# Attention slots of a four-layer kernel: the norms turned one tap earlier, one rotation step on GpSimd, and GpSimd's order changed

## The chip, the cores and the metric

One core of a Trainium2 chip. The metric is the device time of one execution of the whole program, in microseconds; lower is better. The kernel before takes 2851.93 us (median of 3 runs, 2851.05 to 2853.13).

## What is computed

Four post-norm layers on x of shape (4, 512, 512) in float32: a pooled-attention layer, a dense gated FFN, a lagged attention with 16 heads of 128, and a mixture of 8 experts. The change lies in the third. Cut to what matters:

```python
q, k, v = silu(x @ Wq), silu(x @ Wk), silu(x @ Wv)      # z = x @ Wz, a = x @ Wa, b = x @ Wb
q, k, v = (causal_dwconv(u, w) for u, w in ...)          # 4 taps along the sequence
q = q * cos + rot_half(q) * sin                          # rot_half: (-second half, first half)
k = k * cos + rot_half(k) * sin
q = q / maximum(norm(q), 1e-12); k = k / maximum(norm(k), 1e-12)
for s in range(4):                                       # lags
    attn = einsum('bshd,bshd->bsh', q, lag(k, s)) * scale
    out = out + (attn * sigmoid(lag(a, s) * b))[..., None] * lag(v, s)
out = out * rsqrt(mean(out * out) + eps) * norm_w * silu(z)
x = layernorm(x + out @ Wout)
```

## The kernel before

**Slots.** The lagged attention runs as 64 slots, slot f.s = 4 * head + batch (`f.head`, `f.b`). A slot works on four steps at once: f projects and convolves its own step, l1 is the step one slot behind (squares, norms, scores), l2 two behind (mixture, gate, output projection), l3 three behind (its output is added to `x_tok`). Every engine has its own program, written out by hand in the order in which it runs; semaphores join them. Nothing reorders an instruction at run time.

**TensorE in a slot**, in order: 12 matmuls of 512 columns into bank A (first halves of q and k), 12 into B (second halves), the squares and values of l1 turned, `mix(l2)`, `score(l1)`, 12 into A (v), 12 into B (z of l1), 12 of the output projection. The v block waits for the three taps on c1 (`s_c1`), since A must be free, the z block for those on c2 (`s_c2`), and the next slot's first matmul for those on cv (`s_cv`).

**VectorE in a slot**: `accumulate(l3)` four times, `probabilities(l2)` (gate times query norms, out `lag_prob`), three taps on c1, the sums of squares (`norm_sums`, lines L3217 and L3220), the first tap on c2, `gated_output`, two taps on c2, `gains` (L3191), `turn_norms` (L3225), `y_low`, cross2 = c1 * sin (L3483), cross1 = c2 * sin (L3489), three taps on cv, and r1 = r1 - cross1 (L3500).

**GpSimd in a slot**: `band_of_query(l2)` (L2952, the query norms times a band mask, in place), the low parts of the next head's weights (`split_head`, L2941/L2944; two matrices where f.b is 1 or 2, one where it is 3, none where it is 0), the power -1/2 of the norms (L3082), r1 = c1 * cos (L3085), the issue of a DMA that adds l2's squares in DRAM (L2961), r2 = c2 * cos (L3090), r2 = r2 + cross2 (L3093), and the sum of both squares (L3095).

**The query norms travel.** The 1/norm of q is wanted along the other axis, in every partition. `turn_norms` writes it turned; SyncE stores it to DRAM with five small DMAs (`store_query`), waits for their landing, and loads it back broadcast to 128 partitions (`load_query`). Two lines say who waits for it:

```python
def band_of_query(st):
    pool.wait_ge(s_query, st.s * 96 + 96)
...
def probabilities(st):
    dve.wait_ge(s_band, st.s + 1 + (st.s > WHOLE))
```

SyncE's queue then moves r1 and r2 into `rot_q` and `rot_k` by four DMAs (partition halves are regrouped), for the score of the next slot.

Of the kernel before, what the change touches and what calls it, by code (L numbers as in the profile page):

```python
# [86 lines left out]
def until(eng, sem, value):  # L87

    if not isinstance(value, int) or value > 0:
        eng.wait_ge(sem, value)  # L90
# [1700 lines left out]
def layers(nc, mem, a, lag_b, saved, query_norm, square_sums, store):  # L1791
# [16 lines left out]
    with phase(nc) as ctx:  # L1808
# [200 lines left out]
        with nc.Block() as block:  # L2009
            @block.sync  # L2010
            def _(sp):
# [93 lines left out]
                for f, l1, l2, l3 in slots():  # L2105
# [26 lines left out]
                    if l1 and l1.s < BY_ROW:  # L2132
# [3 lines left out]
                        load_query(l1)  # L2136
                    sp.wait_ge(s_rotated, 3 * f.s + 3)
                    until(sp, s_s, f.s)
                    sp.dma_start(rot_q[0:64, 0:SEQ], r1[0:64, :]).then_inc(s_move1, 16)
                    sp.dma_start(rot_k[0:64, :], r1[64:128, :]).then_inc(s_move1, 16)  # L2140
                    sp.wait_ge(s_cos, f.s * 3 + 3)
                    sp.dma_start(rot_q[64:128, 0:SEQ], r2[0:64, :]).then_inc(s_move2, 16)
                    sp.dma_start(rot_k[64:128, :], r2[64:128, :]).then_inc(s_move2, 16)
                    if f.s == 0:
# [345 lines left out]
            def _(act):  # L2490
# [242 lines left out]
                for f, l1, l2, l3 in slots():  # L2733
# [14 lines left out]
                    act.activation(A, A, ACT.Silu).then_inc(s_silu, 1)  # L2748
                    until(act, s_cos, f.s * 3 - 2)
                    until(act, s_rotated, 3 * f.s - 2)  # L2750
                    act.wait_ge(s_silu, f.s * 3 + 1)
# [6 lines left out]
                    act.activation(B, B, ACT.Silu).then_inc(s_silu, 1)  # L2758
                    until(act, s_cos, f.s * 3 - 1)
                    until(act, s_rotated, 3 * f.s - 1)  # L2760
                    act.wait_ge(s_silu, f.s * 3 + 2)
# [172 lines left out]
            def _(pool):  # L2934
# [132 lines left out]
                pool.wait_ge(s_rotation, 32)  # L3067
                for f, l1, l2, l3 in slots():
                    if l2 and l2.s < BY_ROW:
                        band_of_query(l2)  # L3070
                    if f.b and f.head + 1 < HEADS:
                        split_head(f.head + 1, 1 - f.wbuf, SPLIT_AT[f.b])
                    elif f.b == 1:
                        experts.sums(pool, 0)
                        experts.split_lo(pool, 0, 0)
                    elif f.b == 2:
                        pool.wait_ge(s_op, f.head * BATCH * TPB)
                        experts.split_lo(pool, 0, 1)
                        experts.split_lo(pool, 0, 2)
                    if l1:  # L3080
                        pool.wait_ge(s_n2, 3 * l1.s + 2)
                        pool.tensor_tensor(norms[l1.rbuf][:, 0:2 * TPB], norm2, half[:, 0:2 * TPB], ALU.pow).then_inc(s_rn, 1)  # L3082
                    pool.wait_ge(s_c1, f.s * TAPS + TAPS)
                    until(pool, s_move1, f.s * 32)
                    pool.tensor_tensor(r1, c1, cos, ALU.mult).then_inc(s_cos, 1)  # L3085
                    if l2 and l2.s < BY_ROW:
                        add_squares(l2)
                    pool.wait_ge(s_c2, f.s * TAPS + TAPS)
                    until(pool, s_move2, f.s * 32)
                    pool.tensor_tensor(r2, c2, cos, ALU.mult).then_inc(s_cos, 1)  # L3090
                    pool.wait_ge(s_cos, f.s * 3 + 2)
                    pool.wait_ge(s_rotated, 3 * f.s + 1)
                    pool.tensor_tensor(r2, r2, cross2, ALU.add).then_inc(s_cos, 1)  # L3093
                    pool.wait_ge(s_sqr, f.s * 2 + 2)
                    pool.tensor_tensor(squares[0], squares[0], squares[1], ALU.add).then_inc(s_pair, 1)  # L3095
                    if f.s == END - 1:
                        mean_root(0)
                    elif f.s == END:
                        with_residual(0)
# [62 lines left out]
            def _(dve):  # L3162
# [279 lines left out]
                for f, l1, l2, l3 in slots():  # L3442
# [22 lines left out]
                    if l2:  # L3465
                        gated_output(l2)
                    tap(1, f, B, c2, 2, s_c2)
                    tap(1, f, B, c2, 3, s_c2)
                    if l1:
                        gains(l1)  # L3470
                        if f.s == END:
                            probabilities(l1)
                            sum_features(2, OP0)
                        turn_norms(l1)
                    if f.s == 1:
# [3 lines left out]
                    dve.wait_ge(s_c1, f.s * TAPS + TAPS)  # L3479
                    until(dve, s_cos, 3 * f.s)  # L3480
                    if f.s == 0:
# [5 lines left out]
                    dve.wait_ge(s_c2, f.s * TAPS + TAPS)  # L3487
                    until(dve, s_rotated, 3 * f.s)
                    dve.tensor_tensor(cross1, c2, sin, ALU.mult).then_inc(s_rotated, 1)  # L3489
# [6 lines left out]
                    if f.s >= END - 1:  # L3496
                        mean_squares(f.s - (END - 1))
                    dve.wait_ge(s_cos, f.s * 3 + 1)
                    dve.wait_ge(s_rotated, 3 * f.s + 2)
                    dve.tensor_tensor(r1, r1, cross1, ALU.subtract).then_inc(s_rotated, 1)  # L3500
                    if f.s == END:
# [249 lines left out]
```

## Time and profile before

| what | value |
|---|---|
| median of 3 runs | 2851.93 us (2851.05 to 2853.13) |
| the profiled execution's own time | 2859.97 us |
| its span | 2858.2 us |
| busy: PE, PEld, DVE, ACT, POOL | 2821.6, 2322.7, 2307.8, 1445.7, 1683.5 us |
| granted TensorE clock | 0.997 of full speed |
| attention slots | from about 747 to 1830 us |
| 823 to 1762 us: PE, DVE, ACT, POOL busy of 939 us | 933.2, 893.0, 525.4, 614.3 us |

PE busy is a union of overlapping matmuls: one is recorded as 0.39 us long and the next starts 0.227 us after it, so a short pause between two does not show in the busy share. The starts of matmuls tell more.

### The profile page before, as it was taken

To read this page: it belongs to the slowest core of one execution; us is meant where nothing else is said; L and a number is where in the kernel's file an instruction comes from. 1 tells how busy PE (TensorE), PEld (TensorE's weight loads), DVE (VectorE), ACT (ScalarE), POOL (GpSimd) and SP (SyncE) were. 2 spreads that over 40 slices of the span, in tenths; PEclk is the share of its full clock that TensorE was granted. 3 is DMA by queue.
4 is the path that set the end of the run, shared out by engine and by line. 5 is a ranking of instruction groups with operands and counts; after the bars stand their busy time and mean duration, and the time that the engine had idled before them with its cause. 6 is when DMAs were issued, how large, how long until landed. Compare 5 with 4: busy or idle time off the path is not lost.

```text
span 2858.2 us, 39883 instructions
## 1 busy us (share of the span) xinstructions
PE 2821.6 (99%) x13234; PEld 2322.7 (81%) x13234; DVE 2307.8 (81%) x3268; ACT 1445.7 (51%) x2653; POOL 1683.5 (59%) x1204
## 2 busy tenths in 40 slices
PE   9999999999999999999999999899999999999998
PEld 7888888888788888888888888777778887888886
DVE  7899587777899999999999999877667777666665
ACT  6656333333655555555555555564545445444443
POOL 7787233333466666666666666756545556556554
PEclk9999999999999999999999999999999999999999
DMA  3000000000334444444444443321111111211111
GB/s 138 1 23 25 12 19 27 30 27 26 121 98 101 97 97 97 101 97 97 99 99 106 106 104 86 108 74 52 52 45 52 60 45 58 83 45 60 52 52 45
DMA packets 99347, 193.98 MB, mean 68 GB/s; under 512 B 15688, under 2 KB 24264, under 8 KB 98120
## 3 DMA queue, kind: packets, MB, share of 16 engines
q1 hardware_dynamic: 90760, 175.70, 20.7%
q0 software_dynamic: 8384, 15.73, 4.2%
q8 instruction: 108, 1.77, 0.3%
q14 instruction: 95, 0.78, 0.1%
HBM read 133.32 MB, written 24.51 MB: 55 GB/s over the span
## 4 chain that ended last, share of the span: by engine, by line
PE 69%; DVE 13%; DMA 7%; issue 6%; POOL 2%; SPq 2%; ACT 1%; DVEq 0%; ACTq 0%; POOLq 0%
PE OP L45 7%; PE OP L47 7%; PE OP L46 7%; DVE lag_c L3170 4%; DMA lag_query<-query_norm_scratch 4%; DMA query_norm_scratch<-lag_turned 3%; PE S L1470 3%; PE S L1472 3%; PE S L1471 3%; PE A L45 2%; PE A L1470 2%; PE A L1471 2%; PE A L1472 2%; PE A L47 2%; PE A L46 2%
## 5 line engine op out<-in xcount | busy, mean ns | idle before, releaser
L1546 DVE SCALAR_TENSOR_TENSOR x_tok<-OP,expert_weight,x_tok 128x512 f32<-128x512 f32 x252 | 188.1, 748 | 137.4 <-PE OP L47 137.3
L1425 POOL TENSOR_TENSOR middle_w_lo<-second_raw,middle_w_hi 128x512 fp32r<-128x512 f32 (+1 forms) x96 | 143.9, 1500 | 210.2 <-ACT middle_w_hi L1420 210.2
L1518 POOL TENSOR_TENSOR middle_in_lo<-middle_slot,middle_in_hi 128x512 fp32r<-128x512 f32 x128 | 168.7, 1318 | 131.8 <-ACT middle_in_hi L1514 130.9
L3082 POOL TENSOR_TENSOR lag_norms<-lag_norm,minus_half 128x8 f32<-128x8 f32 x63 | 105.0, 1667 | 192.1 <-DVE lag_norm L3220 192.0
L45 PE MATMUL A<-xT_hi,lag_w_hi 128*128 128x512 f32 x512 | 209.9, 410 | 4.0 <-DVE lag_cv L3170 1.7
L45 PE MATMUL B<-xT_hi,lag_w_hi 128*128 128x512 f32 x516 | 204.6, 396 | 5.0 <-DVE lag_c L3170 2.9
L47 PE MATMUL B<-xT_hi,lag_w_lo 128*128 128x512 f32 x516 | 201.4, 390 | 0.0
L46 PE MATMUL B<-xT_lo,lag_w_hi 128*128 128x512 f32 x516 | 201.1, 390 | 0.0
L47 PE MATMUL A<-xT_hi,lag_w_lo 128*128 128x512 f32 x512 | 199.8, 390 | 0.0
L46 PE MATMUL A<-xT_lo,lag_w_hi 128*128 128x512 f32 x512 | 199.7, 390 | 0.0
L45 PE MATMUL OP<-middle_down_hi,middle_in_hi 128*128 128x512 f32 x496 | 193.6, 390 | 1.9 <-POOL middle_down_lo L1445 1.7
L47 PE MATMUL OP<-middle_down_hi,middle_in_lo 128*128 128x512 f32 x496 | 193.1, 389 | 0.0
L46 PE MATMUL OP<-middle_down_lo,middle_in_hi 128*128 128x512 f32 x496 | 193.0, 389 | 0.0
L1425 POOL TENSOR_TENSOR middle_w_lo<-middle_raw,middle_w_hi 128x512 fp32r<-128x512 f32 (+1 forms) x96 | 155.0, 1618 | 64.5 <-ACT middle_w_hi L1420 62.5
L2748 ACT ACTIVATE A<-A 128x512 f32<-128x512 f32 x64 | 37.2, 582 | 278.7 <-PE A L47 278.7
L1263 DVE TENSOR_TENSOR x_tok<-OP,x_tok 128x512 f32<-128x512 f32 x188 | 128.9, 689 | 54.7 <-PE OP L47 54.5
L3170 DVE SCALAR_TENSOR_TENSOR lag_c<-A,lag_conv,lag_c 128x511 f32<-128x511 f32 (+2 forms) x192 | 143.2, 746 | 18.0 <-ACT lag_c L2752 13.2
L1470 PE MATMUL S<-xT_hi,middle_w_hi 128*128 128x512 f32 x384 | 150.4, 392 | 1.5 <-ACT middle_slot L1503 0.8
L1508 ACT ACTIVATE middle_slot<-middle_slot 128x512 f32<-128x512 f32 x128 | 80.8, 632 | 138.9 <-DVE middle_slot L1527 138.8
L1472 PE MATMUL S<-xT_hi,middle_w_lo 128*128 128x512 f32 x384 | 149.5, 389 | 0.0
L2952 POOL TENSOR_TENSOR lag_query<-lag_query,lag_band 128x524 f32<-128x524 f32 x62 | 75.5, 1218 | 122.5 <-DMA lag_query<-query_norm_scratch 122.5
L3170 DVE SCALAR_TENSOR_TENSOR lag_cv<-A,lag_conv,lag_cv 128x511 f32<-128x511 f32 (+2 forms) x192 | 143.0, 745 | 4.6
(706 smaller groups left out, 9286.3 us busy)
## 6 DMA issues: line engine op xcount, KB each, us to landing
lag_raw<-in_head_weights SPq DMA_DIRECT2D x64, 256.0 KB, 4.3
lag_b_row<-lag_b_scratch SPq DMA_DIRECT2D x64, 256.0 KB, 3.3
lag_rot_q<-lag_r SPq DMA_DIRECT2D x128, 128.0 KB, 2.4
lag_rot_k<-lag_r SPq DMA_DIRECT2D x128, 128.0 KB, 2.4
middle_down_raw<-in_expert_down SPq DMA_DIRECT2D x32, 512.0 KB, 3.4
lag_query<-query_norm_scratch SPq DMA_DIRECT2D x62, 262.0 KB
square_sums_scratch<-head_squares POOLq DMA_DIRECT2D x60, 256.0 KB, 4.2
middle_raw<-in_expert_in SPq DMA_DIRECT2D x32, 384.0 KB, 3.0
```

The source lines that it names most:

```text
L45: pe.matmul(out, lh, rh, start=first and k == 0, stop=False)
L46: pe.matmul(out, lh, rl, start=False, stop=False)
L47: done = pe.matmul(out, ll, rh, start=False, stop=last and k == n - 1)
L1263: dve.tensor_tensor(row, self.down_bank(q, n), row, ALU.add).then_inc(self.s_acc, 1)
L1425: pool.tensor_tensor(self.w_lo[q % 2][:, out], self.raw[q % 2][:, of], f32(self.w_hi[q % 2][:, out]), ALU.subtract).then_inc(self.s_wlo, 1)
L1470: pe.matmul(out, w_hi, hi[:, k, :], start=first and k == 0, stop=False, skip_group_check=not first)
L1471: pe.matmul(out, w_hi, lo[:, k, :], start=False, stop=False, skip_group_check=not first)
L1472: done = pe.matmul(out, w_lo, hi[:, k, :], start=False, stop=k == 1, skip_group_check=not first)
L1518: pool.tensor_tensor(self.inner_lo[q % 3][t], self.slot((1, 3)[t], q), f32(self.inner_hi[q % 3][t]), ALU.subtract).then_inc(self.s_lo, 1)
L1546: dve.scalar_tensor_tensor(row, self.down_bank(v, n), self.expert_weight[:, e:e + 1], row, op0=ALU.mult, op1=ALU.add).then_inc(self.s_acc, 1)
L3082: pool.tensor_tensor(norms[l1.rbuf][:, 0:2 * TPB], norm2, half[:, 0:2 * TPB], ALU.pow).then_inc(s_rn, 1)
L3170: dve.scalar_tensor_tensor(out[:, shift:], src[:, 0:SEQ - shift], wj, out[:, shift:], op0=ALU.mult, op1=ALU.add).then_inc(done, 1)
```

## The change

Four things. (1) VectorE turns the norms of l1 between the second and the third tap on c2, where before it did so after the third tap and the gains. (2) r1 = r1 - cross1 moves from VectorE, behind the cv taps, to GpSimd, behind r2 = r2 + cross2; `s_cos` now counts four steps a slot and `s_rotated` two, and all waits follow. (3) GpSimd splits the next head's weights first and masks the query norms after, and issues the DMA of squares after r2 = c2 * cos instead of before it. (4) SyncE moves r2 first and r1 after.

```diff
@@ SyncE
-                    sp.wait_ge(s_rotated, 3 * f.s + 3)
+                    sp.wait_ge(s_cos, f.s * 4 + 3)
                     until(sp, s_s, f.s)
+                    sp.dma_start(rot_q[64:128, 0:SEQ], r2[0:64, :]).then_inc(s_move2, 16)
+                    sp.dma_start(rot_k[64:128, :], r2[64:128, :]).then_inc(s_move2, 16)
+                    sp.wait_ge(s_cos, f.s * 4 + 4)
                     sp.dma_start(rot_q[0:64, 0:SEQ], r1[0:64, :]).then_inc(s_move1, 16)
                     sp.dma_start(rot_k[0:64, :], r1[64:128, :]).then_inc(s_move1, 16)
-                    sp.wait_ge(s_cos, f.s * 3 + 3)
-                    sp.dma_start(rot_q[64:128, 0:SEQ], r2[0:64, :]).then_inc(s_move2, 16)
-                    sp.dma_start(rot_k[64:128, :], r2[64:128, :]).then_inc(s_move2, 16)
@@ GpSimd
+                    if f.b and f.head + 1 < HEADS:
+                        split_head(f.head + 1, 1 - f.wbuf, SPLIT_AT[f.b])
                     if l2 and l2.s < BY_ROW:
                         band_of_query(l2)
-                    if f.b and f.head + 1 < HEADS:
-                        split_head(f.head + 1, 1 - f.wbuf, SPLIT_AT[f.b])
...
                     pool.tensor_tensor(r1, c1, cos, ALU.mult).then_inc(s_cos, 1)
-                    if l2 and l2.s < BY_ROW:
-                        add_squares(l2)
                     pool.wait_ge(s_c2, f.s * TAPS + TAPS)
                     until(pool, s_move2, f.s * 32)
                     pool.tensor_tensor(r2, c2, cos, ALU.mult).then_inc(s_cos, 1)
-                    pool.wait_ge(s_cos, f.s * 3 + 2)
-                    pool.wait_ge(s_rotated, 3 * f.s + 1)
+                    if l2 and l2.s < BY_ROW:
+                        add_squares(l2)
+                    pool.wait_ge(s_cos, f.s * 4 + 2)
+                    pool.wait_ge(s_rotated, 2 * f.s + 1)
                     pool.tensor_tensor(r2, r2, cross2, ALU.add).then_inc(s_cos, 1)
+                    pool.wait_ge(s_rotated, 2 * f.s + 2)
+                    pool.tensor_tensor(r1, r1, cross1, ALU.subtract).then_inc(s_cos, 1)
@@ VectorE
                     tap(1, f, B, c2, 2, s_c2)
+                    if l1:
+                        turn_norms(l1)
                     tap(1, f, B, c2, 3, s_c2)
                     if l1:
                         gains(l1)
...
-                        turn_norms(l1)
...
-                    dve.wait_ge(s_cos, f.s * 3 + 1)
-                    dve.wait_ge(s_rotated, 3 * f.s + 2)
-                    dve.tensor_tensor(r1, r1, cross1, ALU.subtract).then_inc(s_rotated, 1)
```

GpSimd's order before, from the rotation of one slot to that of the next, where the next one splits two matrices (`lag_w_lo10` and `lag_w_lo11` are the low parts, `lag_query` the masked query norms, `lag_norms0` the power):

```order
L3085 TENSOR_TENSOR lag_r1<-lag_c1,lag_cos 128x512
L2961 DMA square_sums_scratch<-head_squares 128x512
L3090 TENSOR_TENSOR lag_r2<-lag_c2,lag_cos 128x512
L3093 TENSOR_TENSOR lag_r2<-lag_r2,lag_cross2 128x512
L3095 TENSOR_TENSOR lag_square0<-lag_square0,lag_square1 128x512
L2952 TENSOR_TENSOR lag_query<-lag_query,lag_band 128x524
L2941 TENSOR_TENSOR lag_w_lo10<-lag_raw0,lag_w_hi10 128x512
L2941 TENSOR_TENSOR lag_w_lo11<-lag_raw1,lag_w_hi11 128x512
L3082 TENSOR_TENSOR lag_norms0<-lag_norm2,minus_half 128x8
```

The same place in the changed kernel:

```order
L3085 TENSOR_TENSOR lag_r1<-lag_c1,lag_cos 128x512
L3088 TENSOR_TENSOR lag_r2<-lag_c2,lag_cos 128x512
L2961 DMA square_sums_scratch<-head_squares 128x512
L3093 TENSOR_TENSOR lag_r2<-lag_r2,lag_cross2 128x512
L3095 TENSOR_TENSOR lag_r1<-lag_r1,lag_cross1 128x512
L3097 TENSOR_TENSOR lag_square0<-lag_square0,lag_square1 128x512
L2941 TENSOR_TENSOR lag_w_lo10<-lag_raw0,lag_w_hi10 128x512
L2941 TENSOR_TENSOR lag_w_lo11<-lag_raw1,lag_w_hi11 128x512
L2952 TENSOR_TENSOR lag_query<-lag_query,lag_band 128x524
L3082 TENSOR_TENSOR lag_norms0<-lag_norm2,minus_half 128x8
```

One instruction more stands there (the new L3095), the two splits stand ahead of the mask instead of behind it, and the DMA's issue has changed places with r2 = c2 * cos.

VectorE's order before, from the c2 taps to the end of a slot:

```order
L3207 SCALAR_TENSOR_TENSOR O<-O,lag_norm,lag_zs 128x512
L3170 SCALAR_TENSOR_TENSOR lag_c<-B,lag_conv,lag_c 128x510
L3170 SCALAR_TENSOR_TENSOR lag_c<-B,lag_conv,lag_c 128x509
L3191 SCALAR_TENSOR_TENSOR lag_gate<-lag_gate,S 128x524
L3225 STREAM_TRANSPOSE lag_turned<-lag_norms 128x32
L3212 TENSOR_TENSOR lag_y_lo<-O,lag_y_hi 128x512
L3483 TENSOR_TENSOR lag_cross<-lag_c,lag_sin 128x512
L3489 TENSOR_TENSOR lag_cross<-lag_c,lag_sin 128x512
L3170 SCALAR_TENSOR_TENSOR lag_cv<-A,lag_conv,lag_cv 128x511
L3170 SCALAR_TENSOR_TENSOR lag_cv<-A,lag_conv,lag_cv 128x510
L3170 SCALAR_TENSOR_TENSOR lag_cv<-A,lag_conv,lag_cv 128x509
L3500 TENSOR_TENSOR lag_r<-lag_r,lag_cross 128x512
```

And in the changed kernel:

```order
L3209 SCALAR_TENSOR_TENSOR O<-O,lag_norm,lag_zs 128x512
L3172 SCALAR_TENSOR_TENSOR lag_c<-B,lag_conv,lag_c 128x510
L3227 STREAM_TRANSPOSE lag_turned<-lag_norms 128x32
L3172 SCALAR_TENSOR_TENSOR lag_c<-B,lag_conv,lag_c 128x509
L3193 SCALAR_TENSOR_TENSOR lag_gate<-lag_gate,S 128x524
L3214 TENSOR_TENSOR lag_y_lo<-O,lag_y_hi 128x512
L3486 TENSOR_TENSOR lag_cross<-lag_c,lag_sin 128x512
L3492 TENSOR_TENSOR lag_cross<-lag_c,lag_sin 128x512
L3172 SCALAR_TENSOR_TENSOR lag_cv<-A,lag_conv,lag_cv 128x511
L3172 SCALAR_TENSOR_TENSOR lag_cv<-A,lag_conv,lag_cv 128x510
L3172 SCALAR_TENSOR_TENSOR lag_cv<-A,lag_conv,lag_cv 128x509
```

The transpose stands one tap and the gains earlier, and the last row is gone.

## Rows read from the trace of the kernel before

**Rows 1.** The page, part 1: busy us, share of the span, instructions.
```profile
PE 2821.6 (99%) x13234; PEld 2322.7 (81%) x13234; DVE 2307.8 (81%) x3268; ACT 1445.7 (51%) x2653; POOL 1683.5 (59%) x1204
```

**Rows 2.** The waits of all engines: us in total, times, longest us.
```profile
PEld B L45 <- DVE lag_c L3170: 14.9, 32, 1.0
PEld A L45 <- DVE lag_cv L3170: 12.6, 29, 0.5
```

**Rows 3.** Timeline of PE: the first matmuls of slots 3, 4, 46, 60, 62.
```profile
806.58 0.39 PE L45 MATMUL A<-xT_hi,lag_w_hi 128*128 128x512 f32 x1
...
822.86 0.39 PE L45 MATMUL A<-xT_hi,lag_w_hi 128*128 128x512 f32 x1
...
1527.32 0.50 PE L45 MATMUL A<-xT_hi,lag_w_hi 128*128 128x512 f32 x1
...
1761.39 0.47 PE L45 MATMUL A<-xT_hi,lag_w_hi 128*128 128x512 f32 x1 [0.17 <-DVE lag_cv L3170]
...
1794.60 0.50 PE L45 MATMUL A<-xT_hi,lag_w_hi 128*128 128x512 f32 x1
```

**Rows 4.** Timeline of PE in slot 46: the last v matmul and the first of z.
```profile
1538.06 0.39 PE L47 MATMUL A<-xT_hi,lag_w_lo 128*128 128x512 f32 x1
1538.29 0.50 PE L45 MATMUL B<-xT_hi,lag_w_hi 128*128 128x512 f32 x1
```

**Rows 5.** Timeline of DVE in slot 46, and the c1 taps of slot 60.
```profile
1530.76 1.68 DVE L3199 TENSOR_TENSOR lag_prob<-lag_gate,lag_query 128x524 f32<-128x524 f32 x1 [0.38 <-POOL lag_query L2952]
1532.36 2.31 DVE L3170 SCALAR_TENSOR_TENSOR lag_c<-A,lag_conv,lag_c 128x511 f32<-128x511 f32 x3
1534.59 0.68 DVE L3217 TENSOR_REDUCE lag_norm<-OP 128x8 f32<-128x512 f32 x1
...
1535.38 0.75 DVE L3170 SCALAR_TENSOR_TENSOR lag_c<-B,lag_conv,lag_c 128x511 f32<-128x511 f32 x1
...
1536.71 1.52 DVE L3170 SCALAR_TENSOR_TENSOR lag_c<-B,lag_conv,lag_c 128x510 f32<-128x510 f32 x2
...
1538.76 0.21 DVE L3225 STREAM_TRANSPOSE lag_turned<-lag_norms 128x32 f32<-128x32 f32 x1
...
1539.45 1.78 DVE L3483 TENSOR_TENSOR lag_cross<-lag_c,lag_sin 128x512 f32<-128x512 f32 x1
1541.15 0.68 DVE L3489 TENSOR_TENSOR lag_cross<-lag_c,lag_sin 128x512 f32<-128x512 f32 x1
1541.75 2.31 DVE L3170 SCALAR_TENSOR_TENSOR lag_cv<-A,lag_conv,lag_cv 128x511 f32<-128x511 f32 x3
1543.98 0.82 DVE L3500 TENSOR_TENSOR lag_r<-lag_r,lag_cross 128x512 f32<-128x512 f32 x1
...
1765.85 2.32 DVE L3170 SCALAR_TENSOR_TENSOR lag_c<-A,lag_conv,lag_c 128x511 f32<-128x511 f32 x3 [0.59 <-ACT lag_c L2752]
```

**Rows 6.** Timeline of POOL in slot 46, to the mask of slot 47.
```profile
1529.42 1.21 POOL L2952 TENSOR_TENSOR lag_query<-lag_query,lag_band 128x524 f32<-128x524 f32 x1 [1.98 <-DMA lag_query<-query_norm_scratch]
1530.59 3.00 POOL L2941 TENSOR_TENSOR lag_w_lo<-lag_raw,lag_w_hi 128x512 fp32r<-128x512 f32 x2
1535.55 1.67 POOL L3082 TENSOR_TENSOR lag_norms<-lag_norm,minus_half 128x8 f32<-128x8 f32 x1 [1.96 <-DVE lag_norm L3220]
1537.21 1.29 POOL L3085 TENSOR_TENSOR lag_r<-lag_c,lag_cos 128x512 f32<-128x512 f32 x1
1538.45 0.89 POOL L2961 DMA_DIRECT2D square_sums_scratch<-head_squares  x1
1539.09 1.58 POOL L3090 TENSOR_TENSOR lag_r<-lag_c,lag_cos 128x512 f32<-128x512 f32 x1
1541.37 1.62 POOL L3093 TENSOR_TENSOR lag_r<-lag_r,lag_cross 128x512 f32<-128x512 f32 x1 [0.70 <-DVE lag_cross L3483]
...
1546.52 1.22 POOL L2952 TENSOR_TENSOR lag_query<-lag_query,lag_band 128x524 f32<-128x524 f32 x1 [2.28 <-DMA lag_query<-query_norm_scratch]
```

More of the change, by code:

```diff
@@ L2748, in _ @@
                     act.activation(A, A, ACT.Silu).then_inc(s_silu, 1)
-                    until(act, s_cos, f.s * 3 - 2)
-                    until(act, s_rotated, 3 * f.s - 2)
+                    until(act, s_cos, f.s * 4 - 3)
+                    until(act, s_rotated, 2 * f.s - 1)
                     act.wait_ge(s_silu, f.s * 3 + 1)
@@ L2758, in _ @@
                     act.activation(B, B, ACT.Silu).then_inc(s_silu, 1)
-                    until(act, s_cos, f.s * 3 - 1)
-                    until(act, s_rotated, 3 * f.s - 1)
+                    until(act, s_cos, f.s * 4 - 2)
+                    until(act, s_rotated, 2 * f.s)
                     act.wait_ge(s_silu, f.s * 3 + 2)
@@ L3068, in _ @@
                 for f, l1, l2, l3 in slots():
+                    if f.b and f.head + 1 < HEADS:
+                        split_head(f.head + 1, 1 - f.wbuf, SPLIT_AT[f.b])
                     if l2 and l2.s < BY_ROW:
                         band_of_query(l2)
-                    if f.b and f.head + 1 < HEADS:
-                        split_head(f.head + 1, 1 - f.wbuf, SPLIT_AT[f.b])
-                    elif f.b == 1:
+                    if f.head + 1 == HEADS and f.b == 1:
                         experts.sums(pool, 0)
                         experts.split_lo(pool, 0, 0)
-                    elif f.b == 2:
+                    elif f.head + 1 == HEADS and f.b == 2:
                         pool.wait_ge(s_op, f.head * BATCH * TPB)
@@ L3479, in _ @@
                     dve.wait_ge(s_c1, f.s * TAPS + TAPS)
-                    until(dve, s_cos, 3 * f.s)
+                    until(dve, s_cos, 4 * f.s - 1)
                     if f.s == 0:
@@ L3487, in _ @@
                     dve.wait_ge(s_c2, f.s * TAPS + TAPS)
-                    until(dve, s_rotated, 3 * f.s)
+                    until(dve, s_cos, 4 * f.s)
                     dve.tensor_tensor(cross1, c2, sin, ALU.mult).then_inc(s_rotated, 1)
```

## The prediction

> **What bounds the kernel now.** I read the page's busy shares first, then the waits, then the starts of matmuls, then the timelines of VectorE and GpSimd in one slot. TensorE is busy 99% of the span [rows 1], but matmuls overlap in the records, so that number hides short pauses; VectorE's 81% is an average over four layers. The waits name the pauses: before the z block TensorE waits for the c2 taps, and before a slot's first matmul for the cv taps, together 27.5 us, both VectorE's work [rows 2]. How much can be had is read from starts. The quiet slot 3 lasts 822.86 - 806.58 = 16.28 us; from slot 3 to slot 62 there are 59 slots in 1794.60 - 806.58 = 988.02 us, 16.75 us each [rows 3]. The same matmuls at the quiet slot's pace would take 59 * 16.28 = 960.5 us, so 27.5 us is what the slots lose. A late start also costs about 0.11 us beyond the wait: the first matmul after one is 0.50 us long where 0.39 is usual [rows 3, 4].
>
> Why VectorE is late shows in slot 46, which starts at 1527.32 and splits two matrices. Two things add up.
>
> First, a loop through DRAM. The mask of the query norms ends at 1529.42 + 1.21 = 1530.63 [rows 6]; VectorE multiplies with it, goes through the taps, and turns the next norms at 1538.76, 8.13 us later [rows 5]; from there to the next mask's start, through store and load, are 1546.52 - 1538.76 = 7.76 us, and GpSimd had been idle 2.28 us when the data came [rows 6]. With the mask's 1.22 us the loop takes 17.11 us against TensorE's 16.28.
>
> Second, blocking between VectorE and GpSimd. `lag_prob` takes 1.68 us while GpSimd splits weights [rows 5, 6]. cross2 takes 1.78 us where its twin cross1 takes 0.68: it ends at 1541.23, 0.56 us after GpSimd's r2 = c2 * cos, which ends at 1539.09 + 1.58 = 1540.67 [rows 5, 6]. And r2 = r2 + cross2 takes 1.62 instead of 1.29 us beside cross1. So where both inputs lie in SBUF, one engine waits until the other's instruction is over, while the taps, which read a bank, keep 0.75 us each. The Trainium skill says the same on its page "SBUF — State Buffer", section "Who interferes with whom": the port pair is an exclusive lock, taken by a VectorE instruction with two SBUF inputs against a GpSimd one that reads SBUF. It weighs against giving GpSimd yet another SBUF operation, but a page's rule has no duration here; the sum below takes the blocked times from the rows.
>
> **The change, costed.** Let E be the time from a slot's start to the end of its mask; slot 46 has E = 3.31. Everything after it follows from start-to-start distances in [rows 5, 6].
>
> VectorE from E: `lag_prob` starts 0.13 us later. In the new order GpSimd is idle then, since the splits are done, so it costs 0.62 to the next start instead of 1.60 (1532.36 - 1530.76): a full 1.0 us off the slots that split. The c1 taps start at E+0.75, the sums of squares at +2.23 = E+2.98, the first c2 tap at +0.79 = E+3.77, the second at +1.33 = E+5.10, the moved transpose at +0.67 = E+5.77, the third tap 0.13 later (its 0.21 us less the usual 0.08 of overlap) and over at E+6.65; z can start 0.06 after that, E+6.71. The transpose needs the power, which ends at E+3.94+1.67 = E+5.61, so it has 0.16 us to spare and waits for nothing.
>
> When z wants to start: 1538.06 + 0.23 - 1527.32 = 10.97 us into slot 46, less the 0.11 of restart in it: 10.86 [rows 3, 4]. So E up to 4.15 costs nothing. An early E gains nothing either, since ScalarE gives c1 only 1765.85 - 1761.39 = 4.46 us into a slot [rows 3, 5], as if E were 3.7.
>
> The loop through DRAM, new: 5.77 + 7.76 + 1.22 = 14.75 us, against 17.11. It no longer binds, with 1.5 us to spare.
>
> GpSimd's own loop, new. From E: the power at +3.94, r1 = c1 * cos at +5.60, r2 = c2 * cos at +6.84 (c2 is ready at 6.65), the DMA's issue at +8.09. That holds GpSimd 0.93 us (from 1538.45 to 1540.67 - 1.29), to +9.02. Meanwhile VectorE reaches cross2 at 6.65 + 1.10 = +7.75 (1539.45 - 1538.23 less the transpose's 0.12), is blocked to +8.13, and ends it at +8.69 and cross1 at +9.29. So r2 = r2 + cross2 works from about +9.2, not +9.02. Then one instruction each 1.25 us: the new r1 = r1 - cross1 at +10.45, squares +11.70, split +12.95, split +14.20, mask +15.45, over at +16.67. With one split the loop is 15.42 us, with none 14.17. The price of the new subtraction, 1.25, is taken from its neighbours' start distance (1.24 between the two instructions from 1537.21); if cross1 blocked it like the addition it would be 1.58.
>
> Chain the slots of a head, each starting P after the one before, and E' = E + loop - P. f.b = 0: E is 3.7 at its floor. f.b = 1: 3.7 + 16.67 - 16.28 = 4.09, z at 10.80, no loss. f.b = 2: 4.09 + 0.39 = 4.48, z at 11.19 instead of 10.86, loss 0.33 + 0.11 = 0.44, P = 16.72. f.b = 3, one split: 3.18, no loss. Back at f.b = 0 GpSimd would give 1.6 and DRAM 3.7 + 14.75 - 16.28 = 2.2, both under the floor. The cv taps end at E + 9.21 + 2.31 = 16.0 even for f.b = 2, before TensorE wants bank A at 16.7: that wait goes in all slots, since the subtraction of 0.82 us [rows 5] is off VectorE and cross2 is blocked for 0.4 instead of 1.1 us.
>
> Losses left: 14 heads * 0.44 = 6.2 us. Gain: 27.5 - 6.2 = 21.3 us; I take 1 us off for transfers that come unusually late, so 20.
>
> At nothing I cost three things. The moves of r1 and r2: r1 is done at E+11.74 = 16.2 even at f.b = 2, where it is 1543.98 + 0.82 - 1527.32 = 17.5 now, so the score is served earlier; without that, a late move would stall TensorE one for one. The sum of squares ends 0.5 us later (17.5) and is turned after 24 matmuls of the next slot, about 22. The slots beyond 62 and the tail: nothing, perhaps a gain of 1 us, as VectorE has one instruction less there.
>
> All of this is in the profiled execution, whose span is 2858.2 and own time 2859.97 us; the median shown is 8 us lower, and I apply the 20 us to the median: 2851.9 - 20 = 2832 us.
>
> **Rivals.** (a) TensorE reaches its pace in all slots: if GpSimd's loop is 0.2 us shorter per slot than I work out (for instance if the addition does not wait for cross1, 9.02 instead of 9.2), f.b = 2 loses little or nothing, gain 27 us, time 2825.
>
> (b) The loop is 0.3 us longer, the subtraction blocked to 1.58: f.b = 1 has E = 4.4 and loses 0.35, f.b = 2 has 4.7 and loses 0.69. 14 heads * 1.04 = 14.6 us lost, gain 13, time 2839.
>
> (c) Slower. The issue of the squares' DMA now falls on cross2 and cross1 (+8.09 to +9.29), where today it falls on taps and gains. No row shows an issue beside an instruction with two SBUF inputs. If those hold it up, it starts at +9.29, ends at +10.2 instead of 9.2, and the loop is 1.0 us longer: f.b = 1: E = 5.1, loss 1.05; f.b = 2: 5.4, loss 1.39; f.b = 3: 4.2, loss 0.14. 14 * 2.58 = 36 us, against 27.5 now: 9 us slower, 2861. It decides from about 0.7 us on. The bounds of the issue's price are 0.93 (free, as now) and 1.93; I take 0.93, nearest to its row. The page named above says in its consequences that a tensor_tensor takes only the read side of the pair, and that descriptor writing needs the write side, an inference of its own; by it (c) does not happen and the sum stays.
>
> (d) No change to speak of: half of (c), or DRAM transfers that come later because load and moves now follow closer. The load has 1.5 us of slack; if it lost 2.5 us, the gain would be mostly gone, time around 2850.
>
> **How the numbers follow.** My case 0.50 (2828 to 2836), (a) 0.18, (b) 0.17, (c) 0.05, (d) 0.08, 0.02 elsewhere. A difference under 0.2% (5.7 us) can't be told from none here. My case, (a) and (b) are faster, with the rest 0.87; (d) is the same, 0.08; (c) slower, 0.05. The range runs from (a) to somewhat beyond (b): 2824 to 2843.
>
> **What the next profile would show.** The waits for lag_cv before A gone, those for lag_c before B left only at f.b = 2. `lag_prob` near 0.7 us everywhere, cross2 near 0.95 to 1.0. The mask waits for DMA only where f.b is 0, and starts at about 3.3 us into a slot at f.b = 2. The DMA's issue stays 0.9 us and the addition starts 0.93 after it; if it starts 1.9 after, (c) is true. The new subtraction shows about 1.29 us; 1.6 means (b). Slots at 16.28, with 16.7 at f.b = 2. I am wrong if the transpose waits for the power (0.16 us to spare, and it would push every third tap), or if the losses before A stay.

## The result, and the profile after

| | kernel before | changed kernel |
|---|---|---|
| median of 4 runs each | 2852.53 us (2851.05 to 2853.79) | 2837.74 us (2837.14 to 2838.06) |
| ratio, 95% interval | | 0.9947 (0.9935 to 0.9959) |
| profiled execution: own time, span | 2859.97, 2858.2 us | 2838.06, 2836.3 us |

The forecast was 2832 us. The gain between the medians is 14.8 us where 20 were expected. Between the two profiled executions (the last row, one execution of each kernel) it is 21.9 us. Why these two differ is taken up in the part on the prediction.

The page's busy line of the changed kernel, to be held against [rows 1]:

```profile
PE 2806.3 (99%) x13234; PEld 2327.4 (82%) x13234; DVE 2168.4 (76%) x3204; ACT 1448.5 (51%) x2653; POOL 1735.1 (61%) x1268
```

64 instructions (the subtractions) went from VectorE to GpSimd. VectorE lost 139 us of busy time: 64 * 0.82 = 52 us are the subtractions, the rest is mostly blocking that is gone (from 823 to 1762 us cross2 fell from a mean of 1.73 to 0.90 us, `lag_prob` from 1.42 to 0.71). The wait of the mask for its load, in the kernel before (us in total, times, longest us):

```profile
POOL lag_query L2952 <- DMA lag_query<-query_norm_scratch: 122.5, 62, 3.6
```

The waits of the changed kernel, to be held against it and against [rows 2]:

```profile
POOL lag_norms L3082 <- DVE lag_norm L3222: 282.1, 63, 6.2
...
DVE lag_prob L3201 <- POOL lag_query L2952: 122.7, 62, 5.0
...
PEld B L45 <- DVE lag_c L3172: 7.6, 20, 0.7
...
POOL lag_query L2952 <- DMA lag_query<-query_norm_scratch: 5.7, 8, 1.7
```

The wait before bank A is gone but for one instance of 1.2 us, that before B is halved, and the mask waits for its load in 8 slots only, where it did in all 62. Slot 46 of the changed kernel starts at 1512.69. First the timeline of PE (start, duration), with the starts of slots 46 and 47 and the first z matmul between them:

```profile
1512.69 0.39 PE L45 MATMUL A<-xT_hi,lag_w_hi 128*128 128x512 f32 x1
...
1523.69 0.50 PE L45 MATMUL B<-xT_hi,lag_w_hi 128*128 128x512 f32 x1
...
1529.31 0.40 PE L45 MATMUL A<-xT_hi,lag_w_hi 128*128 128x512 f32 x1
```

VectorE in it, to be held against [rows 5]:

```profile
1517.14 0.70 DVE L3201 TENSOR_TENSOR lag_prob<-lag_gate,lag_query 128x524 f32<-128x524 f32 x1 [2.87 <-POOL lag_query L2952]
1517.76 2.31 DVE L3172 SCALAR_TENSOR_TENSOR lag_c<-A,lag_conv,lag_c 128x511 f32<-128x511 f32 x3
...
1522.76 0.20 DVE L3227 STREAM_TRANSPOSE lag_turned<-lag_norms 128x32 f32<-128x32 f32 x1
...
1524.76 0.94 DVE L3486 TENSOR_TENSOR lag_cross<-lag_c,lag_sin 128x512 f32<-128x512 f32 x1
1525.62 0.68 DVE L3492 TENSOR_TENSOR lag_cross<-lag_c,lag_sin 128x512 f32<-128x512 f32 x1
```

And GpSimd from the mask of slot 45 to the new subtraction of slot 46, against [rows 6]:

```profile
1499.17 1.21 POOL L2952 TENSOR_TENSOR lag_query<-lag_query,lag_band 128x524 f32<-128x524 f32 x1
...
1513.29 2.54 POOL L2941 TENSOR_TENSOR lag_w_lo<-lag_raw,lag_w_hi 128x512 fp32r<-128x512 f32 x2
1515.79 1.22 POOL L2952 TENSOR_TENSOR lag_query<-lag_query,lag_band 128x524 f32<-128x524 f32 x1
1520.95 1.67 POOL L3082 TENSOR_TENSOR lag_norms<-lag_norm,minus_half 128x8 f32<-128x8 f32 x1 [3.95 <-DVE lag_norm L3222]
...
1525.10 0.88 POOL L2961 DMA_DIRECT2D square_sums_scratch<-head_squares  x1
1525.86 1.61 POOL L3093 TENSOR_TENSOR lag_r<-lag_r,lag_cross 128x512 f32<-128x512 f32 x1
1527.43 1.30 POOL L3095 TENSOR_TENSOR lag_r<-lag_r,lag_cross 128x512 f32<-128x512 f32 x1
```

What to see: `lag_prob` takes 0.70 instead of 1.68 us; cross2 takes 0.94 instead of 1.78. No idle time stands ahead of the mask, so the load is in before GpSimd asks for it: from mask to mask, 1515.79 - 1499.17 = 16.62 us, GpSimd's loop sets the pace, with the 4 us in it in which GpSimd waits for VectorE's sums of squares. z starts late, and the slot lasts 1529.31 - 1512.69 = 16.62 instead of 16.28.

Slot lengths, worked out from the first matmul of each slot and averaged for slots 8 to 55 by f.b (0, 1, 2, 3): before 16.47, 16.88, 16.87, 16.91; after 16.33, 16.46, 16.56, 16.33 us. Over slots 2 to 61 the mean fell from 16.740 to 16.414, 60 * 0.326 = 19.6 us, and 2.3 us more came from what follows, 1.2 of them from slot 62.

### The profile page after: what moved, and what is told of

It is laid out like the page before. It is cut to its first block, busy times and chain, and to the rows that moved or that the text cites. A ratio compares the mean times of both kernels' runs of the same rounds, so it can differ in the third digit from the quotient of the medians.

```text
span 2836.3 us, 39819 instructions
## 1 busy us (share of the span) xinstructions
PE 2806.3 (99%) x13234; PEld 2327.4 (82%) x13234; DVE 2168.4 (76%) x3204; ACT 1448.5 (51%) x2653; POOL 1735.1 (61%) x1268
## 4 chain that ended last, share of the span: by engine, by line
PE 86%; DVE 5%; POOL 3%; issue 2%; DMA 2%; ACT 2%; SPq 0%; POOLq 0%; DVEq 0%; ACTq 0%
PE OP L45 7%; PE OP L47 7%; PE OP L46 7%; PE B L45 4%; PE A L45 4%; PE A L47 4%; PE A L46 4%; PE B L47 4%; PE B L46 4%; PE S L1470 3%; PE S L1472 3%; PE S L1471 3%; PE A L1470 2%; PE A L1471 2%; PE A L1472 2%
## 5 line engine op out<-in xcount | busy, mean ns | idle before, releaser
L3172 DVE SCALAR_TENSOR_TENSOR lag_c<-B,lag_conv,lag_c 128x511 f32<-128x511 f32 (+2 forms) x192 | 142.6, 743 | 0.1
```

Of the source, the lines that this page charges most:

```text
L3172: dve.scalar_tensor_tensor(out[:, shift:], src[:, 0:SEQ - shift], wj, out[:, shift:], op0=ALU.mult, op1=ALU.add).then_inc(done, 1)
```

## Experiments

Two theories stand in the expectations. The loop theory is that of the prediction: two loops, one through DRAM and one of GpSimd's own work, are held against TensorE's 16.28 us. The work theory says that time follows the work taken off VectorE. Times are medians, ratios are to the kernel before run beside, with a 95% interval. The experiments came in four sets, each on another chip, and the kernel before took 2858.64, 2857.55, 2852.71 and 2857.08 us in them. The changed kernel took 2837.74 and 2838.05 us in two sets; where a run is held against it from another set, this near equality is what the comparison rests on.

Below, E is again the time from a slot's start to the end of its mask, and "load to mask" the time from the issue of the load of the query norms to the start of the mask, a mean over slots 8 to 56.

### One part alone in the kernel before

**Only the transpose.** The norms are turned between the second and third c2 tap.

```diff
                     tap(1, f, B, c2, 2, s_c2)
+                    if l1:
+                        turn_norms(l1)
                     tap(1, f, B, c2, 3, s_c2)
...
-                        turn_norms(l1)
```

> The kernel before with only the norms turned one tap and the gains earlier. Loop theory (what costs time before is the way of the query norms through DRAM, 17.1 us a slot against TensorE's 16.28): the way gets 1.4 us shorter and no longer binds; VectorE, with the subtraction still on it and still blocked by the splits, needs about 16.2 us a slot, so little is left: 2836 to 2841 us. Work theory (VectorE simply has too much to do, and what helps is that 0.82 us leave it): VectorE's work is the same, so 2850 to 2853 us.

2835.43 us (2834.09 to 2837.28), ratio 0.9919 (0.9905 to 0.9934). Two moved lines give as much as the whole change, or 2 to 3 us more. Its waits:

```profile
POOL lag_query L2952 <- DMA lag_query<-query_norm_scratch: 22.9, 29, 1.5
...
DVE lag_prob L3199 <- POOL lag_query L2952: 3.4, 2, 2.2
...
PEld A L45 <- DVE lag_cv L3170: 2.1, 11, 0.3
```

No wait before B is left. `lag_prob` and cross2 are still blocked, as the groups from 900 to 1735 us show (count, busy us, mean ns):

```profile
L3484 DVE TENSOR_TENSOR lag_cross<-lag_c,lag_sin 128x512 f32<-128x512 f32 x52 | 92.5, 1779 | 0.0
...
L3199 DVE TENSOR_TENSOR lag_prob<-lag_gate,lag_query 128x524 f32<-128x524 f32 x51 | 55.1, 1080 | 0.0
```

So VectorE's blocked time costs next to nothing once the loop through DRAM is shorter than a slot: the slots' mean is 16.34 us here, and 16.33 in the kernel below in which neither instruction is blocked to speak of (2832.91 us, 2.5 less than here, with other edits too). VectorE's work is the same as before and 23 us are gone, so the work theory falls.

**Only r1.** The subtraction goes to GpSimd and SyncE moves r2 first; mask, splits, squares' DMA and transpose stay as before.

```diff
-                    dve.tensor_tensor(r1, r1, cross1, ALU.subtract).then_inc(s_rotated, 1)
...
+                    pool.wait_ge(s_rotated, 2 * f.s + 2)
+                    pool.tensor_tensor(r1, r1, cross1, ALU.subtract).then_inc(s_cos, 1)
```

> The kernel before with only r1 = r1 - cross1 given to GpSimd and SyncE moving r2 first; norms turned late, mask ahead of the splits, the DMA of squares ahead of r2 = c2 * cos. Loop theory: the way through DRAM is as long as before, the mask waits for the data as before, 2849 to 2853 us; TensorE's waits for cv go, those for c2 grow. Work theory: this is the part that helps, 2838 to 2841 us.

2902.46 us (2898.12 to 2903.01), ratio 1.015 (1.0135 to 1.0165): far slower than either theory had it. Its waits, and then SyncE's queue in a slot that starts at 1172.5:

```profile
DVE lag_prob L3201 <- POOL lag_query L2952: 129.7, 62, 3.8
...
POOL lag_query L2952 <- DMA lag_query<-query_norm_scratch: 101.2, 61, 3.4
...
PEld B L45 <- DVE lag_c L3172: 43.1, 49, 1.0
```

```profile
1183.67 1.28 SPq L2029 DMA_DIRECT2D query_norm_scratch<-lag_turned  x4
1184.99 0.53 SPq L2030 DMA_DIRECT2D query_norm_scratch<-lag_turned  x1
1187.85 0.34 SPq L2035 DMA_DIRECT2D lag_query<-query_norm_scratch  x1
1188.31 0.47 SPq L2139 DMA_DIRECT2D lag_rot_q<-lag_r  x1
1188.82 0.60 SPq L2140 DMA_DIRECT2D lag_rot_k<-lag_r  x1
1189.46 0.60 SPq L2142 DMA_DIRECT2D lag_rot_q<-lag_r  x1
1190.40 0.46 SPq L2143 DMA_DIRECT2D lag_rot_k<-lag_r  x1
```

The moves wait behind the load in SyncE's program and now are ready when it leaves: the first follows 0.46 us after it. Load to mask is 4.12 us, against 3.24 in the kernel before, where the first move follows 1.73 us after the load. The way through DRAM becomes 8.12 (mask's end to transpose) + 4.36 (transpose to load's issue) + 4.12 + 1.21 (mask) = 17.8 us; the slots' mean is 17.46.

**The same, with the moves held back** until GpSimd's sum of squares is done:

```diff
                     until(sp, s_s, f.s)
+                    sp.wait_ge(s_pair, f.s + 1)
                     sp.dma_start(rot_q[64:128, 0:SEQ], r2[0:64, :]).then_inc(s_move2, 16)
```

> The run with only r1 on GpSimd, which came out at 2902 us, with one more wait: SyncE moves r2 and r1 only after the sum of squares, that is at least 2.5 us later. Crowding theory (the four moves, sent 0.44 us behind the load of the query norms instead of 1.73 us, hold up that load, from 3.24 to 4.11 us, and the loop through DRAM with it): the load is back at 3.2 to 3.4 us and the time at 2850 to 2862 us, like the kernel before. Rival (it is GpSimd's extra 1.25 us or the later sum of squares that costs the 44 us): the time stays at 2895 us or above.

2854.25 us (2852.33 to 2856.46), ratio 0.9989 (0.998 to 0.9998), 48 us less than without the wait; load to mask is 3.18 us again. That the moves crowd the load is shown, since the later wait is the only edit between the two. With the crowding gone, r1 on GpSimd alone is worth about 3 us.

**Only the splits ahead of the mask.**

```diff
+                    if f.b and f.head + 1 < HEADS:
+                        split_head(f.head + 1, 1 - f.wbuf, SPLIT_AT[f.b])
                     if l2 and l2.s < BY_ROW:
                         band_of_query(l2)
-                    if f.b and f.head + 1 < HEADS:
-                        split_head(f.head + 1, 1 - f.wbuf, SPLIT_AT[f.b])
```

> The kernel before with only GpSimd's splits ahead of the mask. Loop theory: the multiplication with the query norms is no longer blocked by a split (1.0 us shorter in 3 of 4 slots), the way through DRAM takes 16.1 us in all slots and hardly binds, GpSimd's own loop is 16.3: 2834 to 2843 us. Rival (a split ahead of the mask only delays it by up to 2.5 us, and GpSimd becomes the bound): 2850 us or more.

2845.94 us (2844.38 to 2847.31), ratio 0.9958 (0.9946 to 0.997), 3 us above the range. TensorE's wait before z falls from 14.9 to 4.5 us, as expected; that before A stays at 12.7: cross2 still takes 1.72 us, since the squares' DMA still pushes r2 = c2 * cos onto it. With the transpose alone cross2 is blocked as much and the wait before A is 2.1 us, but E is 1.65 us there in the median and 3.78 here. So the block seems to cost time only where the mask ends late.

### One part taken back from the changed kernel

**The changed kernel again**, in another set of runs.

> The changed kernel once more, on the chip of this group. The kernel before took 2852 us on one chip and 2859 us on another. Loop theory: before, the way through DRAM bound, so a chip's transfers showed in the time; changed, it has over 1 us to spare, so the time stays 2836 to 2839 us whatever the kernel before takes here. Rival (the chips differ in everything alike): the ratio stays 0.995, so 2844 us where before takes 2859.

2838.05 us (2837.28 to 2838.38), ratio 0.993 (0.9918 to 0.9943). The same time, beside a kernel before that took 5 us more (2857.55 instead of 2852.53 us).

**The subtraction back on VectorE**, behind the cv taps; SyncE moves r1 first again. Run twice.

```diff
-                    pool.wait_ge(s_rotated, 2 * f.s + 2)
-                    pool.tensor_tensor(r1, r1, cross1, ALU.subtract).then_inc(s_cos, 1)
...
+                    dve.wait_ge(s_cos, f.s * 3 + 1)
+                    dve.wait_ge(s_rotated, 3 * f.s + 2)
+                    dve.tensor_tensor(r1, r1, cross1, ALU.subtract).then_inc(s_rotated, 1)
```

> The changed kernel, but with r1 = r1 - cross1 still on VectorE behind the cv taps (norms turned early, splits first, DMA of squares after r2 = c2 * cos). Loop theory: GpSimd's loop is 1.25 us shorter, 15.4 us even with two splits, so TensorE loses nothing for c2, and VectorE has room for the 0.82 us: 2828 to 2833 us, faster than the changed kernel's 2838. Work theory: the subtraction back on VectorE costs most of the gain, 2845 us or more.

> The same kernel as c_r1_on_dve (changed, but the subtraction still on VectorE), beside the changed kernel on one chip: 2832 to 2835 us, 3 to 6 us under the changed kernel; the work theory's 2845 us has fallen already.

2832.91 us (2832.34 to 2834.93), ratio 0.9911 (0.9895 to 0.9928), and 2832.96 us (2832.54 to 2833.75), ratio 0.9913 (0.99 to 0.9927), 5.1 us under the changed kernel on the same chip. Slots last 16.33 us in the mean for every f.b, and TensorE waits for taps only once, 1.2 us. Of the parts of the change, r1's move (with SyncE's order, which goes with it) costs 5 us. This is the fastest kernel of the study.

Its slots also show what TensorE needs by itself: three or four slots of 16.28 us and as many of 16.37 take turns, with one of 16.32 or 16.33 between them, 16.325 in the mean of slots 3 to 61. The prediction took slot 3's 16.28 for all. Why the two kinds of slot differ by 0.09 us was not looked into.

**The splits dealt out otherwise**: two, one, two matrices for f.b = 1, 2, 3.

```diff
-    SPLIT_AT = {1: (0, 1), 2: (2, 3), 3: (4,)}
+    SPLIT_AT = {1: (0, 1), 2: (2,), 3: (3, 4)}
```

> The changed kernel, but the five matrices of the next head are split 2, 1, 2 over f.b = 1, 2, 3 instead of 2, 2, 1. Loop theory: GpSimd's loop is over 16.28 us only with two splits, by 0.4 us, and one such slot between quiet ones is absorbed; the losses of 0.3 us at f.b = 2 go, 15 heads: 3 to 5 us faster than the changed kernel, 2833 to 2835 us. Work theory: the work of every engine is the same, so the time is the same as the changed kernel's, 2837 to 2838 us.

2835.18 us (2834.32 to 2835.39), ratio 0.9918 (0.9903 to 0.9932). That is 2.6 to 2.9 us under the changed kernel, where 3 to 5 were expected. The loss at f.b = 2 goes (16.33 us), f.b = 1 has 16.39. Two long GpSimd slots in a row were the loss at f.b = 2, as the chain of E values has it.

**The squares' DMA back in front of r2 = c2 * cos.**

```diff
+                    if l2 and l2.s < BY_ROW:
+                        add_squares(l2)
                     pool.wait_ge(s_c2, f.s * TAPS + TAPS)
...
                     pool.tensor_tensor(r2, c2, cos, ALU.mult).then_inc(s_cos, 1)
-                    if l2 and l2.s < BY_ROW:
-                        add_squares(l2)
```

> The changed kernel, with the DMA of squares issued again in front of r2 = c2 * cos; all else of the change stays. Loop theory: r2's multiplication runs from E+7.8 to E+9.0, cross2, ready at E+7.75, is held up until then, and the addition follows 0.5 to 1.0 us later than now; GpSimd's loop grows from 16.65 to 17.2 to 17.7 us, the slots with one, two or three quarters of the head behind lose 0.9 to 1.7 us a head more: 2846 to 2862 us, with cross2 near 1.8 us and waits before A back. Rival (only the norms' way and the splits count, the issue's place doesn't): 2835 to 2841 us.

2867.39 us (2865.82 to 2868.25), ratio 1.0048 (1.0031 to 1.0065): slower than the kernel before. cross2's group from 900 to 1735 us, and two waits:

```profile
L3486 DVE TENSOR_TENSOR lag_cross<-lag_c,lag_sin 128x512 f32<-128x512 f32 x50 | 91.1, 1822 | 0.0
```

```profile
PEld B L45 <- DVE lag_c L3172: 27.1, 30, 1.0
...
PEld A L45 <- DVE lag_cv L3172: 12.4, 28, 0.5
```

cross2 is held up 0.9 us and the addition with it. In the medians of f.b = 1, the addition starts 9.73 us after the mask's end here and 8.83 in the changed kernel, so GpSimd's loop is 0.90 us longer (17.52 instead of 16.63 from mask to mask), within what was expected. The time is 5 us above the range, because its sum priced the late z alone: the cv taps are late too, and cost 12 us before A, as in [rows 2].

**The transpose back behind the gains.**

```diff
-                    if l1:
-                        turn_norms(l1)
                     tap(1, f, B, c2, 3, s_c2)
                     if l1:
                         gains(l1)
...
+                        turn_norms(l1)
```

> The changed kernel, with the norms turned again behind the third c2 tap and the gains; all else of the change stays. Loop theory: from the mask's end the late transpose stands 1.0 us later, so the way through DRAM takes about 6.8 + 3.1 + 4.1 to 4.8 + 1.2 = 15.2 to 15.9 us, still under TensorE's 16.28, and GpSimd's own 16.65 goes on setting the slots that split two: 2836 to 2842 us. Rival (the place of the transpose is worth what it was worth alone, 23 us, wherever it is taken away): 2850 us or more.

2848.12 us (2845.59 to 2850.47), ratio 0.9984 (0.9975 to 0.9994). A miss by 6 us: the transpose comes 7.15 us after the mask's end, not 6.8 (a tap and the gains are 1.40 us, not 1.0), and the load takes 4.97 us to the mask. 7.15 + 3.14 + 4.97 + 1.21 = 16.47 us, over TensorE's 16.33: the DRAM loop binds again, and the mask waits for its load in 38 slots instead of 8.

```profile
POOL lag_query L2952 <- DMA lag_query<-query_norm_scratch: 50.9, 38, 3.6
```

The moves now follow the load by a mean of 0.55 us. In the changed kernel the early transpose is needed, though worth 10 us and not 23.

**The mask back ahead of the splits.**

```diff
+                    if l2 and l2.s < BY_ROW:
+                        band_of_query(l2)
                     if f.b and f.head + 1 < HEADS:
                         split_head(f.head + 1, 1 - f.wbuf, SPLIT_AT[f.b])
-                    if l2 and l2.s < BY_ROW:
-                        band_of_query(l2)
```

> The changed kernel, with the query norms masked again ahead of the splits; all else of the change stays. Loop theory: the two splits (2.5 us) leave GpSimd's way from one mask to the next, and fall into the time in which it waits for the sums of squares. The mask starts 0.4 to 0.7 us into a slot by GpSimd (c1 at 4.46, squares over 12.2 later at 16.7) and by the load (transpose 9.5, load issued 3.1 later, 4.0 to 4.4 to the mask); lag_prob is held up by the splits again (1.6 us instead of 0.7) and still ends before ScalarE has c1, so no slot loses: 2829 to 2834 us. Rival (splits ahead of the mask are needed, as they alone were worth 12 us in the kernel before): 2842 us or more.

2841.56 us (2841.41 to 2843.94), ratio 0.9946 (0.9929 to 0.9962). Both theories missed, the rival's "2842 or more" by 0.4 us only. Slots of f.b = 0, 2 and 3 last 16.33 us as the loop theory has it, those of f.b = 1 last 16.93. The worst of them starts at 1168.5. SyncE's queue in the slot ahead of it (f.b = 0), then GpSimd and VectorE in it:

```profile
1158.08 1.85 SPq L2016 DMA_DIRECT2D lag_raw<-in_head_weights  x4
1159.97 0.43 SPq L2017 DMA_DIRECT2D lag_raw<-in_head_out  x1
1161.85 1.28 SPq L2029 DMA_DIRECT2D query_norm_scratch<-lag_turned  x4
1163.17 0.27 SPq L2030 DMA_DIRECT2D query_norm_scratch<-lag_turned  x1
1166.39 0.34 SPq L2035 DMA_DIRECT2D lag_query<-query_norm_scratch  x1
1166.85 0.47 SPq L2139 DMA_DIRECT2D lag_rot_q<-lag_r  x1
```

```profile
1172.19 1.21 POOL L2952 TENSOR_TENSOR lag_query<-lag_query,lag_band 128x524 f32<-128x524 f32 x1 [3.44 <-DMA lag_query<-query_norm_scratch]
```

```profile
1173.53 1.67 DVE L3201 TENSOR_TENSOR lag_prob<-lag_gate,lag_query 128x524 f32<-128x524 f32 x1 [3.84 <-POOL lag_query L2952]
```

In f.b = 0 SyncE also issues the five loads of the next head's weights (256 KB each, 4.4 to 5.0 us to landing). They are in flight when the norms are stored: the load's issue comes a median of 3.95 us after the first store there, 2.43 us at f.b = 1. The load itself is long too, and this time the weights are not what differs: load to mask is 4.84 us in the median of the 14 such slots in which the mask waited for it, and 3.39 in those of the kernel with the transpose alone, which has the same weights in flight. There the first move follows the load by 2.86 us and the squares' DMA leaves 3.5 us ahead of it; here it is 0.46 us and 2.0 us. How the 1.45 us divide between moves and squares was not tried. In the slot shown the mask starts 3.7 us into the slot, and `lag_prob`, blocked by the splits, ends 6.7 us into it, 2.2 us after c1 could be taken. With the splits first, the same late load is covered by 2.5 us of GpSimd work and `lag_prob` takes 0.70. So the order of splits and mask is worth 3.5 us (against the changed kernel's 2838.05 of another set), by a way that the prediction did not have.

### How much the kernel before varies

> The kernel before, unchanged, with a profile of its own on this chip. If its time differs from chip to chip by the DRAM loop, its profiled span stands within 4 us of its time here and the way from the turned norms to the mask's start differs from the 7.76 us of the first profile as the slot's mean does from 16.74 us. If the profiled execution itself is longer than unprofiled ones, the span stands 6 us or more over the runs of the same kernel beside it.

2849.73 us, span 2847.9, with 2852.71 us (2848.32 to 2857.07) of other runs beside it. The two waits of [rows 2] in this profile:

```profile
PEld A L45 <- DVE lag_cv L3170: 10.1, 26, 0.5
...
PEld B L45 <- DVE lag_c L3170: 7.9, 19, 0.8
```

18.0 us instead of 27.5. From the transpose to the mask's start it is 7.28 us in the mean, 7.54 in the first profile; the means of slots 2 to 61 are 16.565 and 16.740. The 60 slots are 10.5 us shorter, and the span is 10.3 us shorter, so the difference between the two executions lies in the slots, where the way through DRAM differs by 0.25 us. The span is near the time of the unprofiled runs beside it, so being profiled does not make an execution long.

Over all sets the kernel before took 2848.3 to 2861.9 us in 46 runs, the changed kernel 2837.1 to 2838.4 in 9. Part of that is from chip to chip (medians of 2852.71 to 2858.64 us on four chips), part within one set (2848.3 to 2857.1). The other kernels sort the same way: where the mask waits for its load in most slots, one set spreads over 4.1 to 4.9 us (r1 alone, the same with late moves, the transpose put back); in the changed kernel, in that with the other split and in the two sets with the subtraction on VectorE it spreads over 0.9 to 2.6 us; the rest lie at 2.4 to 3.2. Sets have 4 to 15 runs. What makes the transfers themselves slower or faster stays open.

## Why the prediction came out as it did

**What bounds the kernel before: right.** The transpose alone gives 23 us, so the loop through DRAM was the bound. The prediction has blocking as a second thing that adds up with it. The runs show it as a part of the loop: with the transpose moved, the blocked time is still there and costs next to nothing; with the splits moved, 1.0 us of it leaves the loop and the kernel gains 12 us.

**The timings after E: right.** At f.b = 1, 2, 3 E is 3.95, 4.29 and 3.11 us in the median (said: 4.09, 4.48, 3.18); the transpose stands at E+5.76 (5.77) and does not wait for the power, which ends 0.14 us ahead of it (0.16); GpSimd's loop with two splits is 16.62 us (16.67); the subtraction takes 1.30 us (1.29).

**Rival (c) is false.** In slot 46 the DMA's issue runs from 1525.10 for 0.88 us beside cross2 and cross1, and the addition starts 0.76 us after its start, so cross2 and cross1 did not hold the issue up. The Trainium skill's page "SBUF — State Buffer", section "Who interferes with whom", infers this (a tensor_tensor leaves the write side to descriptor writing); the trace agrees. It is the addition that cross1 holds up: it takes 1.61 us instead of 1.29.

**The losses: both terms off, in opposite directions.** Of the 27.5 us, 59 * (16.325 - 16.28) = 2.7 us was no lateness, but TensorE's own pace; 24.8 us could be had. From slot 3 to slot 62 the changed kernel lasts 967.8 us, 20.2 less than before, and 4.6 us of lateness are left, where 6.2 were forecast: 16.56 us a slot at f.b = 2 (16.72 said), 16.46 at f.b = 1 (16.28 said). Slot 2 became 0.6 us longer and what follows slot 62's start 2.3 us shorter, where nothing or 1 us was said. So the sum of 21.3 us comes near the measured 21.9 in part by luck: the slots gave less than said, the end gave more.

**The loss at f.b = 1** was put at nothing because the transfers were taken to last 7.76 us as in the kernel before. There that holds for every f.b (7.65, 7.52, 7.50 and 7.47 us in the mean). In the changed kernel it does not at f.b = 0: in the five slots in which the load held up the mask of the next slot, load to mask is 5.4 us in the median, on top of 4.1 us for the stores. The first move follows that load by 0.44 us, and the weights are in flight. Those five are the slots of f.b = 1 from 8 on that last 0.1 to 0.6 us too long. In all, the mask waits for its load in 8 slots, 5.7 us.

**The step that failed: "I apply the 20 us to the median".** The span fell by 21.9 us, from 2858.2 to 2836.3; the sum said 21.3, or 20 with a reserve. The median fell by 14.8. The 27.5 us of loss belonged to the profiled execution. In a run of the kernel before with a span of 2847.9 the same two waits are 18.0 us, and the changed kernel, which no longer waits for DRAM in most slots, takes 2838 us every time. The right sum takes the gain from the execution on which it was read: 2859.97 - 21.3 = 2838.7 us against 2837.74 measured. The mis-sized term is the loss of the median run. That run has no profile, so what follows is an estimate: it is 7.4 us shorter than the profiled one, which would leave it 24.8 - 7.4 = 17.4 us of lateness; 4.6 remain, slot 2 takes 0.6, the end gives 2.3, together 14.5 us against 14.8 measured.

**"At nothing: moves of r1 and r2": wrong in general, and mostly covered here.** Issued right behind the load they delay it by 0.9 us (rival (d) had this). In the changed kernel the first follows 2.0 us after the load at f.b = 1, 2 and 3, but 0.5 at f.b = 0, and a wait of the mask shows in 8 slots only, since the DRAM loop had about 1.5 us to spare. Only once the transpose is put back does it bind.

## What to carry to other kernels

In these runs a kernel bound by a loop through DRAM varied from execution to execution, and the one that was not stayed within 1.3 us; a gain worked out from a profile is taken off that profile's own time, not off a median. Before moving work between two engines that both look busy, find the loop that closes last and shorten that: here two moved lines gave all of it, and the work moved to GpSimd cost 5 us. Where several parts are changed at once, take each one back singly: what a part is worth alone (r1 +44 us, or -3 with the moves held back, transpose -23) says little of what it is worth in company (r1 +5, transpose -10, squares' DMA -29).

## What the runs showed of the hardware beyond expectation

Transfers issued behind a load delay it. Four moves of 128 KB of which the first starts 0.44 us behind a load of 262 KB add 0.9 us to it (4.12 instead of 3.24 us to the mask); 1.7 us behind they add nothing that shows, since 2.5 us behind it is 3.18. The moves suffer too: those to `rot_q` take 3.6 us to landing in the kernel with r1 alone and 2.3 with the moves held back. In the changed kernel the squares' DMA also leaves closer to the load, 0.3 to 1.9 us ahead of it (medians by f.b) instead of 4.5 to 4.8 in the kernel before, and is slower itself. Sizes and median us from issue to landing, first of the kernel with the transpose alone, then of the changed one:

```profile
lag_rot_q<-lag_r SPq DMA_DIRECT2D x128, 128.0 KB, 2.4
...
square_sums_scratch<-head_squares POOLq DMA_DIRECT2D x60, 256.0 KB, 4.1
```

```profile
lag_rot_q<-lag_r SPq DMA_DIRECT2D x128, 128.0 KB, 3.5
...
square_sums_scratch<-head_squares POOLq DMA_DIRECT2D x60, 256.0 KB, 5.5
```

The Trainium skill's page "DMA: Bandwidth & Descriptors", section "Issuing engines are not separate DMA queues", says that transfers of all engines end up on the same 16 DMA engines and interleave; these rows agree: the moves leave from SyncE and the squares from GpSimd, and both are slower where they are close to each other and to the load.

Five small stores of 0.5 KB or less, followed by their landing, take 3.1 to 3.2 us in the mean from transpose to load issue where the squares' DMA leaves GpSimd behind r2 = c2 * cos, and 4.2 to 4.4 where it leaves in front of it with the transpose late (4.3 in the kernel before). With the transpose early and the DMA in front it is 3.28. So the small stores are quick when they are out ahead of the 256 KB of squares, but for the slots with weights in flight (4.1 us at f.b = 0 of the changed kernel, 2.7 to 2.8 at the others). This was read from means, not tried by itself.
